# Preparing the weights of a four-layer graph network in pieces among the first turns

## The chip, the cores and the metric

The kernel runs on one core of a Trainium2 chip. The metric is the device time of one execution in microseconds (us); less is better. The core has a matrix engine (TensorE, here PE), and VectorE (DVE), ScalarE (ACT) and GpSimd (POOL) for everything else. SyncE (SP) issues the DMAs. Each engine works through its own list of instructions in order, and they meet at semaphores.

## The reference, cut to what matters

128 graphs of 128 nodes with 512 features each go through four layers of graph attention. Each layer normalises, takes the positive part, computes attention scores between nodes under a mask from `adj`, takes a softmax, multiplies by it, and adds the result to `x`:

```python
# layer 0:  one head; scores from h @ (W.T a1), h @ (W.T a2)
h = jnp.maximum(_layernorm(x), 0.0);  x = x + elu(softmax(masked(leaky(f1 + f2.T))) @ h)
# layer 1:  two GAT layers: 512 -> 4 heads x 256 (W1, att_src1, att_dst1, b1), elu,
#           then 1024 -> 512, one head (W2, att_src2, att_dst2, b2)
h = jnp.maximum(_layernorm(x), 0.0);  x = x + gat(elu(gat(h, W1, ...)), W2, ...)
# layer 2:  one head, additive attention with attn_w_src, attn_w_dst, attn_b
# layer 3:  8 heads of 64: xp = h @ W_proj; a_src, a_dst = xp . W_att; relu(att @ xp)
```

The weights `W1`, `W2` and `W_proj` are the same for all graphs.

## The kernel before

**Turns.** The kernel is a software pipeline that somebody wrote out by hand. A loop runs over `G + SKEW` turns (`G` = 128 graphs, `SKEW` = 12). In turn `step` each engine runs a fixed list of stages, and a stage called with `t.graph(k)` works on graph `step - k`, if there is one. So graph 0 is loaded in turn 1, meets its layer 0 in turns 2 to 4, its projection by `W1` in turns 4 and 5 (`L1a`), the one by `W2` in turn 6 (`L1b`), layer 2 in turns 7 and 8, the projection by `W_proj` in turn 10 (`L3`), and is stored in turn 12. The order in which an engine runs the stages of a turn is the order of the lines in its loop. Nothing is rearranged later.

**The weights.** They arrive in 16 chunks of 128 rows: chunks 0 to 3 are `w1` (1024 columns), 4 to 11 `w2` (512 columns), 12 to 15 `w3`, which is `W_proj` (512 columns). A chunk is loaded into a staging buffer by `stage_weights` (SP), and then prepared by a `split_weights` on each of three engines:

- DVE multiplies it with the attention vectors and sums, which gives the extra columns `ext`: a dot product (an instruction with its read of the accumulator behind it) for each head and vector. That is 8 for a `w1` chunk (256 wide), 2 for `w2` (512 wide), 16 for `w3` (64 wide).
- ACT copies the chunk to its rounded half `w_hi`, then waits for `ext_made` and copies `ext` also.
- POOL waits for both copies, subtracts them (`w_lo`), and raises `w_split`.

`split_weights(t)` stands first in a turn on each of the three engines. It prepares the chunks in `prepared[t.step]`: before, chunks 0 to 3 in turn 0, 4 to 11 in turn 1, 12 and 13 in turn 2, 14 and 15 in turn 3. The dot products put their products into `scratch`, which is the buffer that the scores of layer 0 use too, and so wait for `st_made0` as well. The staging buffers (`stage`, `stage3`, `att1`, `att2`, `att3`) are buffers of later layers that are still free: `xl` and `g1` of layer 1, `eE`, `pE`, `pTE` and `t_all["L3"]` of layer 3.

**What stands around it.** `load` (SP) brings `x` and `adj` of a graph. `norm_0` (ACT, lines 768 and 778) normalises it, `columns_L0` (DVE, 1112) makes the two score columns, `send_L0` and `spread_L0` (SP, 261 and 283) send the targets through DRAM to all partitions, `masked_L0` (POOL), `leaky_L0`, `exp_L0` (ACT) follow, `turn_exp_L0` and `product_L0` (PE, 396 and 409) turn the result and multiply. `pT_L0` (ACT, 811) copies it from PSUM between these two, and is the first stage of a turn on ACT. `residual_L0` (DVE, 1171) adds `x`. `project_L1a_high` and `_low` (PE, 365) follow `product_L0` on PE, and `values_L1a` (DVE, 1226, `xl`) follows these.

Before the loops, PE multiplies `a0_w` (1 MB) with the vectors of layer 0; POOL's first instruction waits for `setup_pool`, which `offdiag` raises in DVE's `make_rows`, behind the split of turn 0.

Of the kernel before, what the change touches and what calls it, by code (L numbers as in the profile page):

```python
# [1533 lines left out]
```

## Time and profile before

| | us |
|---|---|
| median of 3 runs | 3216.89 (3214.66 to 3220.53) |
| the profiled execution | 3215.87 |
| its span | 3213.9 |
| PE busy | 3052.3 (95%) |
| DVE, ACT, POOL busy | 2436.3, 2413.6, 2116.7 |
| granted TensorE clock, mean | 0.976 |
| `adj_in`, median from issue to landing (page, part 6) | 2.6 |

In the page's picture of 40 slices PE is at 1 in the first slice of 80 us, at 6 and 8 in the next two, at 9 up to the last two. So the kernel has a start, a long even part, and an end.

### The profile page before, as it was taken

What the parts mean: (1) busy time and instruction counts of PE and PEld (TensorE: products, weight loads), DVE (VectorE), ACT (ScalarE), POOL (GpSimd) and SP (SyncE); (2) the same over time, 40 slices, a digit from 0 to 9 for tenths busy, and PEclk for the clock granted to TensorE, in tenths of its full rate; (3) what the DMA queues carried; (4) which work ended last, traced back from release to release, by engine and by line L of the source; (5) the groups of instructions that cost most, each with busy time, mean ns of one, the idle gap of its engine ahead of it and who ended that gap; (6) DMA issues with size and microseconds to landing.
All of it is one profiled execution on the core that took longest, in us unless ns stands there. A gap on an engine that the chain in (4) does not pass through costs nothing.

```text
span 3213.9 us, 77726 instructions
## 1 busy us (share of the span) xinstructions
PE 3052.3 (95%) x21776; PEld 2809.7 (87%) x21776; DVE 2436.3 (76%) x5995; ACT 2413.6 (75%) x6561; POOL 2116.7 (66%) x3236
## 2 busy tenths in 40 slices
PE   1689999999999999999999999999999999999984
PEld 0579999999999999999999999999999999999974
DVE  6477877878787787878778787887878788787752
ACT  2467778878787787877878787887878788787753
POOL 4346666766666676766767666666766677676643
PEclk6899999999999999999999999999999999999986
DMA  4112222222222222222222222222212222222211
GB/s 135 32 46 62 78 63 74 66 64 76 63 78 63 69 71 62 78 63 78 63 69 71 62 78 63 77 64 67 74 62 78 63 75 65 69 72 62 66 39 44
DMA packets 170069, 217.14 MB, mean 68 GB/s; under 512 B 34864, under 2 KB 100528, under 8 KB 169648
## 3 DMA queue, kind: packets, MB, share of 16 engines
q1 hardware_dynamic: 169648, 212.18, 22.2%
q8 instruction: 184, 3.01, 0.4%
q14 instruction: 237, 1.94, 0.2%
HBM read 177.55 MB, written 34.54 MB: 66 GB/s over the span
## 4 chain that ended last, share of the span: by engine, by line
PE 91%; issue 4%; DVE 1%; POOL 1%; ACT 1%; DMA 0%; POOLq 0%; DVEq 0%; ACTq 0%
PE bank_c L365 23%; PE bank_b L365 22%; PE bank_e L365 11%; PE bank_e L691 8%; PE bank_b L513 7%; PE bank_a L409 3%; PE bank_e L655 3%; PE bank_c L591 3%; PE bank_a L435 3%; PE bank_b L507 2%; PE bank_b L358 2%; PE bank_e L358 2%; PE bank_a L396 0%; PE bank_a L422 0%; PE bank_c L579 0%
## 5 line engine op out<-in xcount | busy, mean ns | idle before, releaser
L365 PE MATMUL bank_b<-w_hi,hT_hi 128*128 128x344 f32 x1536 | 470.1, 360 | 7.2 <-DVE hT_lo L1215 6.7
L365 PE MATMUL bank_c<-w_hi,g_hi 128*128 128x258 f32 x2048 | 413.2, 283 | 2.4 <-DVE x L1171 2.4
L365 PE MATMUL bank_c<-w_lo,g_hi 128*128 128x258 f32 x2048 | 413.2, 283 | 0.0
L365 PE MATMUL bank_b<-w_lo,hT_hi 128*128 128x344 f32 x1536 | 410.2, 321 | 0.0
L1474 POOL TENSOR_TENSOR eE<-eE,nmE 128x512 f32<-128x512 f32 x256 | 266.2, 1040 | 178.0 <-DVE nmE L1289 177.0
L1467 POOL TENSOR_TENSOR eE<-t_all_L,mask 128x512 f32<-128x512 f32 x256 | 349.0, 1384 | 32.3 <-DMA t_all_L<-t_dram_L 31.5
L1455 POOL TENSOR_TENSOR g_lo<-g,g_hi 128x512 fp32r<-128x512 f32 x128 | 193.9, 1515 | 262.0 <-ACT g_hi L901 262.0
L365 PE MATMUL bank_c<-w_hi,g_lo 128*128 128x258 f32 x2048 | 363.8, 289 | 0.7
L940 ACT ACTIVATE eE<-eE,st 128x128 f32<-128x128 f32 x1024 | 326.1, 391 | 40.5 <-POOL eE L1467 40.4
L365 PE MATMUL bank_b<-w_hi,hT_lo 128*128 128x344 f32 x1536 | 347.2, 321 | 0.0
L365 PEld LDWEIGHTS bank_b<-w_hi,hT_hi 128*128 128x128 f32 x1536 | 277.7, 189 | 75.0 <-issue 67.1
L365 PEld LDWEIGHTS bank_c<-w_hi,g_hi 128*128 128x128 f32 x2048 | 322.8, 190 | 3.2 <-issue 3.2
L768 ACT ACTIVATE h<-x,rs 128x512 f32<-128x512 f32 x384 | 311.1, 811 | 14.0 <-POOL rs L1386 11.0
L365 PEld LDWEIGHTS bank_c<-w_lo,g_hi 128*128 128x128 f32 x2048 | 318.0, 190 | 0.0
L1383 POOL TENSOR_TENSOR rs<-rs,nhalf 128x1 f32<-128x1 f32 x512 | 289.8, 566 | 42.7
L1381 POOL TENSOR_SCALAR rs<-mv 128x1 f32<-128x1 f32 x512 | 113.0, 221 | 310.5 <-DVE mv L1071 278.6
L365 PE MATMUL bank_e<-w_hi,hT_hi 128*128 128x264 f32 x1024 | 300.6, 309 | 6.2 <-DVE rE L1314 6.2
L365 PEld LDWEIGHTS bank_c<-w_hi,g_lo 128*128 128x128 f32 x2048 | 289.5, 189 | 9.7 <-DVE g_lo L1258 4.3
L1112 DVE CUSTOM_DVE_ANT_0 product<-h,t_row 128x512 bf16<-128x512 f32 x256 | 295.0, 1152 | 0.0
L513 PE MATMUL bank_b<-pTB,xl 128*128 128x128 f32 x2048 | 275.4, 278 | 4.1 <-ACT pTB L880 4.1
L365 PE MATMUL bank_e<-w_lo,hT_hi 128*128 128x264 f32 x1024 | 276.7, 285 | 0.0
L365 PEld LDWEIGHTS bank_b<-w_lo,hT_hi 128*128 128x128 f32 x1536 | 274.2, 189 | 0.0
(136 smaller groups left out, 8785.5 us busy)
## 6 DMA issues: line engine op xcount, KB each, us to landing
t_all_L<-t_dram_L SPq DMA_DIRECT2D x128, 512.0 KB, 3.9
x_in<-in_x SPq DMA_DIRECT2D x128, 256.0 KB, 2.5
t_all_L1a<-t_dram_L1a SPq DMA_DIRECT2D x128, 256.0 KB, 4.3
out<-out_sb SPq DMA_DIRECT2D x128, 256.0 KB, 4.2
t_all_L<-t_dram_L SPq DMA_DIRECT2D x256, 64.0 KB, 2.9
adj_in<-in_adj SPq DMA_DIRECT2D x128, 64.0 KB, 2.6
t_dram_L1a<-t_rows_L1a SPq DMA_DIRECT2D x512, 0.5 KB
t_all_L1b<-t_dram_L1b SPq DMA_DIRECT2D x128, 64.0 KB, 2.8
```

The lines of the kernel that those rows point to most:

```text
L358: last = nc.tensor.transpose(bank[:, c * P:(c + 1) * P], src[:, c * P:(c + 1) * P], ident[:])
L365: last = mm(bank[:, 0:width], a[:, c * P:(c + 1) * P], w[:, c, b * width:(b + 1) * width], start=(first and c == chunks[0] and n == 0), st ...
L513: last = mm(bank_b[:, i, at * P:(at + 1) * P], xl[:, c * P:(c + 1) * P], pTB[:, c * P // F1, :], start=(at == 0), stop=(at == C1 // 2 - 1))
L691: last = mm(bank_e[:, i, k * KA:k * KA + NMIN], pTE[:, head, :], xa[:, head * KA:head * KA + NMIN], start=True, stop=True)
L768: activation(h[layer][:], src, ACT.Relu, bias=rs[layer][:, 2:3], scale=rs[layer][:, 1:2])\
L940: last = activation(eE[:, k, :], eE[:, k, :], ACT.Prelu, bias=st3[:, 0, k:k + 1], alpha=SLOPE)
L1112: last = nc.vector.tensor_tensor_reduce(product[:, layer + i, :], h[layer][:], row[layer][:], 1.0, first, ALU.mult, ALU.add, col)
L1381: ts(v, mv[layer][:, 1:2], EPS, None, ALU.add).then_inc(sem(f"var_made{layer}"), 1)
L1383: tt(r, v, nhalf[:], ALU.pow).then_inc(sem(f"rstd_made{layer}"), 1)
L1455: tt(g_lo[:, half, :], g1[:, half, :], g_hi[:, half, :].bitcast(F32), ALU.subtract)\
L1467: tt(eE[:, half, :], t_all["L3"][:, half, :], m, ALU.add).then_inc(sem(f"L3_masked{i}"), 1)
L1474: tt(eE[:, half, :], eE[:, half, :], nm, ALU.add).then_inc(sem(f"L3_shifted{i}"), 1)
```

## The change

The change does four things.

1. All stages run one turn earlier (`SKEW` = 11, each `t.graph(k)` becomes `t.graph(k - 1)`). Graph 0 is loaded before the loop.
2. The chunks are spread over more turns: 0 to 3 in turn 0, 4 and 5 in turn 1, 6 and 7 in turn 2, 8 to 11 in turn 3, and one of 12 to 15 in each of the turns 5 to 8. SP issues their loads by a table of its own (`fetched`).
3. They are staged in buffers of layer 3 (`eE`, `t_all["L3"]`, `pE`, `pTE`), but for chunks 2 and 3; so two waits of layer 1 for `W2_DONE` become `W1_DONE`.
4. The loads before the loop come in another order (`ident` and `a0_w` first), and `identb` and `offdiag` are made before the split.

```diff
-SKEW = 12
+SKEW = 11
...
-        stage = [xl[:, 0:D1], g1[:].rearrange("p c n -> p (c n)"),
-                 eE[:].rearrange("p h n -> p (h n)"), t_all["L3"][:].rearrange("p h n -> p (h n)")]
+        wide3 = [w.rearrange("p h n -> p (h n)") for w in (eE[:], t_all["L3"][:], pE[:], pTE[:])]
+        stage1 = [wide3[0], wide3[1], xl[:, 0:D1], g1[:].rearrange("p c n -> p (c n)")]
+        stage2 = [w[:, i * D:(i + 1) * D] for w in wide3 for i in range(2)]
...
-        prepared = {0: range(0, C), 1: range(C, C + C1), 2: range(C + C1, C + C1 + C // 2),
-                    3: range(C + C1 + C // 2, len(w_chunks))}
-        staged = [stage[n % WR] if n < C + C1 else stage3[n - C - C1] for n in range(len(w_chunks))]
+        prepared = {0: range(0, C), 1: range(C, C + 2), 2: range(C + 2, C + 4), 3: range(C + 4, C + C1),
+                    5: range(C + C1, C + C1 + 1), 6: range(C + C1 + 1, C + C1 + 2),
+                    7: range(C + C1 + 2, C + C1 + 3), 8: range(C + C1 + 3, C + C1 + C)}
+        fetched = {1: range(C + 4, C + 5), 2: range(C + 5, C + 7), 3: range(C + 7, C + C1),
+                   4: range(C + C1, C + C1 + 1), 5: range(C + C1 + 1, C + C1 + 3), 6: range(C + C1 + 3, C + C1 + C)}
+        staged = stage1 + stage2 + stage2[0:C]
...
-                    if kind == "w2":
+                    if n >= WR:
                         sp.wait_ge(sem("w_split"), n - WR + 1)
-                    if kind == "w3":
-                        sp.wait_ge(sem("w_split"), C + C1)
                     if n == C + C1:
+                        sp.wait_ge(sem("w_split"), C + 6)
...
-            spread(att1[1][:, 0:D1], row(att_src1.rearrange("h f -> (h f)")), "att1_in")
-            spread(att1[0][:, 0:D1], row(att_dst1.rearrange("h f -> (h f)")), "att1_in")
-            stage_weights(range(0, 1))
-
+            sp.dma_start(ident[:], ident_in).then_inc(sem("ident_loaded"), 16)
...
+            spread(att1[1][:, 0:D1], row(att_src1.rearrange("h f -> (h f)")), "att1_in")
+            spread(att1[0][:, 0:D1], row(att_dst1.rearrange("h f -> (h f)")), "att1_in")
+            stage_weights(range(0, 1))
+            load_graph(0, 0)
             stage_weights(range(1, C))
...
                 t = Turn(G, step)
-                if t.step == 1:
-                    load_rest()
-                if t.step in prepared and t.step:
-                    stage_weights(prepared[t.step])
-                spread_L3(t.graph(11))
...
-                load(t.graph(1))
+                if t.step == 0:
+                    stage_weights(range(C, 2 * C))
+                stage_weights(fetched.get(t.step, ()))
+                spread_L3(t.graph(10))
...
+                load(t.graph(0))
...
                     if g.i == 0:
-                        act.wait_ge(sem("w_split"), W2_DONE)
+                        act.wait_ge(sem("w_split"), W1_DONE)
...
             dve.wait_ge(sem("ext_zero"), 1)
+            dve.wait_ge(sem("ident_loaded"), 16)
+            nc.vector.tensor_copy(identb[:], ident[:]).then_inc(sem("setup_pe"), 1)
+            ts(offdiag[:], ident[:], -1.0, 1.0, ALU.mult, ALU.add).then_inc(sem("setup_pool"), 1)
...
-                    dve.wait_ge(sem("st_made0"), t.graph(3).made(1))
+                    dve.wait_ge(sem("st_made0"), t.graph(2).made(1))
```

The first place is ACT's list around `norm_0` of graph 0 (`h<-x_in`) and the first `pT_L0` (`pT_L`). Before:

```order
L761 ACTIVATE w_hi<-pE 128x2x256 [waits w_in3]
L763 ACTIVATE w_hi<-ext 128x2x8 [waits ext_made]
L768 ACTIVATE h<-x_in,rs 128x512 [waits L0_out,rs_made0]
L799 ACTIVATE e_L<-e_L,st 128x128 [waits L0_masked]
L805 ACTIVATE p_L,sum_L<-e_L,nm_L 128x128 [waits L0_recip,L0_turned,L0_max]
L811 ACTIVATE pT_L<-bank_a 128x128 [waits L0_out,L0_turned]
```

The same place of the changed kernel:

```order
L762 ACTIVATE w_hi<-ext 128x4 [waits ext_made]
L767 ACTIVATE h<-x_in,rs 128x512 [waits L0_out,rs_made0]
L798 ACTIVATE e_L<-e_L,st 128x128 [waits L0_masked]
L804 ACTIVATE p_L,sum_L<-e_L,nm_L 128x128 [waits L0_recip,L0_turned,L0_max]
L760 ACTIVATE w_hi<-pE 128x512 [waits w_in0]
L762 ACTIVATE w_hi<-ext 128x4 [waits ext_made]
L760 ACTIVATE w_hi<-pE 128x512 [waits w_in1]
L762 ACTIVATE w_hi<-ext 128x4 [waits ext_made]
L760 ACTIVATE w_hi<-pTE 128x512 [waits w_in2]
L762 ACTIVATE w_hi<-ext 128x4 [waits ext_made]
L760 ACTIVATE w_hi<-pTE 128x512 [waits w_in3]
L762 ACTIVATE w_hi<-ext 128x4 [waits ext_made]
```

`norm_0` of graph 0 had 16 chunks ahead of it and now has 8; four chunks now stand between the exponential and the copy `pT_L`, which follows them.

The second place is the border to the turn in which PE first projects by `W2` (turn 6 before, turn 5 now), on ACT. Before:

```order
L893 ACTIVATE g<-g 128x512 [waits elu_exp0]
L811 ACTIVATE pT_L<-bank_a 128x128 [waits L0_out,L0_turned]
L901 ACTIVATE g_hi<-g 128x512 [waits L1b_xl,g_made_last]
L901 ACTIVATE g_hi<-g 128x512 [waits L1b_first_high,g_made_first]
L768 ACTIVATE h<-x_in,rs 128x512 [waits L0_out,rs_made0]
```

And of the changed kernel:

```order
L892 ACTIVATE g<-g 128x512 [waits elu_exp0]
L760 ACTIVATE w_hi<-eE 128x2x256 [waits w_in0]
L762 ACTIVATE w_hi<-ext 128x2x8 [waits ext_made]
L810 ACTIVATE pT_L<-bank_a 128x128 [waits L0_out,L0_turned]
L900 ACTIVATE g_hi<-g 128x512 [waits L1b_xl,g_made_last]
L900 ACTIVATE g_hi<-g 128x512 [waits L1b_first_high,g_made_first]
L767 ACTIVATE h<-x_in,rs 128x512 [waits L0_out,rs_made0]
```

A chunk of `w3`, with its wait for DVE's dot products, has come between the turns; the same stands in the three turns behind.

The third place is SP's list behind the sending of graph 0's targets of `L1a`. Before:

```order
L269 DMA t_dram_L1a<-t_rows_L1a 4x32 x3
L283 DMA t_all_L1a<-t_dram_L1a 128x512 [waits L1a_masked,L1a_sent]
L254 DMA x_in<-in_x 128x512 [waits mask_made,x1_made]
```

And of the changed kernel:

```order
L269 DMA t_dram_L1a<-t_rows_L1a 4x32 x3
L224 DMA pE<-in_L_gnn_W_att 128x8x64 [waits w_split]
L224 DMA pE<-in_L_gnn_W_att 128x8x64
L226 DMA eE<-in_L_gnn_W_proj 128x512
L283 DMA t_all_L1a<-t_dram_L1a 128x512 [waits L1a_masked,L1a_sent]
L230 DMA x_in<-in_x 128x512 [waits mask_made,x1_made]
```

Three loads now stand ahead of the spread `t_all_L1a` of graph 0.

## Rows read from the trace of the kernel before

**Rows 1.** Busy time by stretch: us, then busy us and count by engine, granted clock

```profile
254.00:3088.00 2834.00, 2832.77 (x20534) 2625.02 (x20532) 2248.16 (x5414) 2254.70 (x6151) 1961.94 (x3004) 1.00 0.23 69
```

**Rows 2.** The chain that ended last, first 260 us: start, us, what

```profile
24.00 55.77 issue
...
142.55 0.86 PE bank_a L409 x2
...
163.95 0.99 PE bank_a L409 x2
...
186.16 0.86 PE bank_a L409 x2
```

**Rows 3.** Timeline, turn 0: start, us, engine, line, operation, [idle before, releaser]

```profile
13.37 0.42 DVE L1041 CUSTOM_DVE_ANT_0 product<-g,pE 128x256 bf16<-128x256 f32 x1 [2.72 <-DMA g<-in_L_gnn_W]
...
16.14 0.08 DVE L1041 DVE_READ_ACCUMULATOR2_ANT ext<- 128x1 f32 x1
...
22.87 2.34 POOL L1372 TENSOR_TENSOR w_lo<-xl,w_hi 128x1024 fp32r<-128x1024 f32 x1 [22.44 <-DVE offdiag L1053]
```

**Rows 4.** DMAs of the first 60 us: size, median us from issue to landing

```profile
ident<-in_ident SPq DMA_DIRECT2D x1, 64.0 KB, 6.8
```

**Rows 5.** Timeline, turn 1, dot products of `w2` beside POOL's subtractions

```profile
28.15 2.53 DVE L1041 CUSTOM_DVE_ANT_0 product<-xl,h 128x512 bf16<-128x512 f32 x1 [4.16 <-DMA xl<-in_L_gnn_W]
...
34.80 1.53 DVE L1041 CUSTOM_DVE_ANT_0 product<-eE,h 128x512 bf16<-128x512 f32 x1
...
37.08 1.53 DVE L1041 CUSTOM_DVE_ANT_0 product<-t_all_L,h 128x512 bf16<-128x512 f32 x1
```

**Rows 6.** Timeline, turn 3, `norm_0` of graph 0 on ACT

```profile
70.43 0.80 ACT L768 ACTIVATE h<-x_in,rs 128x512 f32<-128x512 f32 x1
```

**Rows 7.** Timeline, border of turns 3 and 4, DVE's last and PE's first

```profile
79.70 0.16 DVE L1166 RECIPROCAL sum_L<-sum_L 128x1 f32<-128x1 f32 x1
...
80.73 2.05 PE L409 MATMUL bank_a<-h,pT_L 128*128 128x512 f32 x2 [0.52 <-ACT pT_L L811]
```

**Rows 8.** Timeline, one `w3` chunk: its load, and its dot products on DVE

```profile
51.07 1.01 SPq L224 DMA_DIRECT2D pTE<-in_L_gnn_W_att  x2
...
56.59 0.23 DVE L1041 CUSTOM_DVE_ANT_0 product<-eE,pTE 128x64 bf16<-128x64 f32 x1 [7.46 <-DMA eE<-in_L_gnn_W_proj]
...
58.92 0.09 DVE L1041 DVE_READ_ACCUMULATOR2_ANT ext<- 128x1 f32 x1
```

**Rows 9.** Timeline, turn 5, the targets of `L1a` of graph 0

```profile
97.64 0.34 SPq L283 DMA_DIRECT2D t_all_L1a<-t_dram_L1a  x1
...
100.88 1.23 DVE L1226 TENSOR_TENSOR xl<-bank_b,b_row 128x1032 f32<-128x1032 f32 x1 [1.72 <-issue]
101.06 1.16 POOL L1442 TENSOR_TENSOR eB<-t_all_L1a,mask_turned 128x512 f32<-128x512 f32 x1 [9.37 <-DMA t_all_L1a<-t_dram_L1a]
```

**Rows 10.** Timeline, border of turns 5 and 6

```profile
120.73 1.10 PE L409 MATMUL bank_a<-h,pT_L 128*128 128x512 f32 x2 [1.61 <-ACT pT_L L811]
121.01 0.15 DVE L1166 RECIPROCAL sum_L<-sum_L 128x1 f32<-128x1 f32 x1
```

**Rows 11.** Timeline, DVE's last instruction of the turns 6, 7 and 8

```profile
142.77 0.75 DVE L1171 SCALAR_TENSOR_TENSOR x<-bank_c,sum_L1b,x 128x512 f32<-128x512 f32 x1 [0.77 <-PE bank_c L591]
...
164.80 0.75 DVE L1171 SCALAR_TENSOR_TENSOR x<-bank_c,sum_L1b,x 128x512 f32<-128x512 f32 x1
...
186.60 0.75 DVE L1171 SCALAR_TENSOR_TENSOR x<-bank_c,sum_L1b,x 128x512 f32<-128x512 f32 x1
```

**Rows 12.** Busy time by stretch, start and end of the kernel; granted clock after POOL's

```profile
114.00:118.00 4.00, 4.00 (x16) 4.00 (x16) 0.76 (x3) 0.79 (x3) 0.00 (x0) 0.50 0.02 4
...
122.00:126.00 4.00, 4.00 (x28) 4.00 (x28) 3.30 (x6) 0.75 (x1) 2.41 (x3) 1.00 0.36 102
...
3092.00:3096.00 4.00, 1.64 (x11) 1.63 (x11) 3.20 (x6) 2.11 (x7) 3.53 (x3) 0.89 0.32 111
3096.00:3100.00 4.00, 4.00 (x26) 4.00 (x25) 2.26 (x4) 3.06 (x9) 2.70 (x4) 0.68 0.07 16
```

More of the change, by code:

```diff
@@ L748, in _ @@
-                product_L2(t, t.graph(8))
-                turn_exp_L1b(t, t.graph(6))
-                project_L3_first(t, t.graph(10))
-                turn_exp_L0(t, t.graph(3))
+                product_L1b(t, t.graph(6))
+                product_L0(t, t.graph(3))
+                project_L1a_high(t, t.graph(4))
+                project_L1a_low(t, t.graph(4))
+                project_L1b_first_high(t, t.graph(5))
+                turn_h3(t, t.graph(9))
+                project_L1b_first_low(t, t.graph(5))
@@ new lines, in _ @@
+                project_L1b_last(t, t.graph(5))
+                turn_exp_L3_last(t, t.graph(10))
+                turn_exp_L3_first(t, t.graph(10))
+                turn_prob_L1a(t, t.graph(4))
+                product_L3_last(t, t.graph(10))
+                product_L3_first(t, t.graph(10))
+                product_L1a_last(t, t.graph(4))
+                turn_h1(t, t.graph(3))
+                turn_mask(t, t.graph(3))
+                project_L3_last_high(t, t.graph(9))
+                project_L3_last_low(t, t.graph(9))
@@ L753, in _ @@
+                turn_exp_L2(t, t.graph(7))
+                project_L1a_last(t, t.graph(3))
+                product_L1a_first(t, t.graph(4))
+                product_L2(t, t.graph(7))
+                turn_exp_L1b(t, t.graph(5))
+                project_L3_first(t, t.graph(9))
+                turn_exp_L0(t, t.graph(2))
         @block.scalar
@@ L1050, in make_rows @@
                 if t.step == 0:
-                    dve.wait_ge(sem("ident_loaded"), 16)
-                    nc.vector.tensor_copy(identb[:], ident[:]).then_inc(sem("setup_pe"), 1)
-                    ts(offdiag[:], ident[:], -1.0, 1.0, ALU.mult, ALU.add).then_inc(sem("setup_pool"), 1)
                     dve.wait_ge(sem("u0_made"), 1)
@@ L1347, in _ @@
-                rows_L3(t.graph(10))
-                recip_L2(t.graph(8))
-                most_L0(t.graph(3))
-                most_L1b(t.graph(6))
-                rows_L1a(t.graph(4))
-                elu_L1a_last(t.graph(5))
-                stats_0(t.graph(1))
-                residual_L2(t.graph(8))
-                recip_L1b(t.graph(6))
-                elu_L1a_first(t.graph(5))
-                recip_L0(t.graph(3))
-                columns_L2(t.graph(7))
-                residual_L1b(t.graph(6))
+                rows_L2(t.graph(7))
@@ new lines, in _ @@
+                sources_L3(t.graph(10))
+                residual_L0(t.graph(3))
+                columns_L0(t.graph(2))
+                values_L1a(t.graph(4))
+                moments_0(t.graph(1))
+                g_lo_first(t.graph(5))
+                rows_L0(t.graph(2))
+                most_L3_last(t.graph(10))
+                most_L1a(t.graph(4))
+                most_L3_first(t.graph(10))
+                hT_lo_L3(t.graph(9))
+                stats_1(t.graph(3))
+                recip_L1a(t.graph(4))
@@ new lines, in _ @@
+                moments_1(t.graph(3))
+                stats_3(t.graph(8))
+                rows_L1b(t.graph(5))
+                values_L1b(t.graph(5))
+                stats_2(t.graph(6))
+                recip_L3(t.graph(10))
+                result_L3(t.graph(10))
+                most_L2(t.graph(7))
+                moments_3(t.graph(8))
+                moments_2(t.graph(6))
+                hT_lo_L1a(t.graph(3))
+                rows_L3(t.graph(9))
+                recip_L2(t.graph(7))
+                most_L0(t.graph(2))
@@ L1361, in _ @@
+                most_L1b(t.graph(5))
+                rows_L1a(t.graph(3))
+                elu_L1a_last(t.graph(4))
+                stats_0(t.graph(0))
+                residual_L2(t.graph(7))
+                recip_L1b(t.graph(5))
+                elu_L1a_first(t.graph(4))
+                recip_L0(t.graph(2))
+                columns_L2(t.graph(6))
+                residual_L1b(t.graph(5))
         @block.gpsimd
```

195 lines of the change are left out of this document (73 added, 122 removed).

## The prediction, made before the changed kernel ran

> **What bounds the kernel now.** I read the busy time by stretch first. From 254 to 3088 us PE is busy for 2832.77 of 2834.00 us at a full clock [rows 1]. Nothing that the change does reaches into that part: after turn 8 every engine has the list that it had, and what is computed per graph is the same. So only the start can pay, and a microsecond by which the even part begins earlier is a microsecond of the span. The chain of waits shows the start next: after the weights' first dot products it has 55.77 us of "issue" that end with graph 0's first use of PE, near 80 us [rows 2]. There the engines DVE, ACT and POOL prepare 16 chunks, and the first `norm_0` waits behind all of them. Behind it the pipeline fills: the chain passes through `product_L0` (bank_a L409) once per turn, at 142.55, 163.95 and 186.16, that is every 21.4 to 22.2 us. These turns are bound by one loop over PE, DVE, ACT and POOL, which PE's in-order list closes: `product_L0`, `project_L1a`, `xl`, softmax, `product_L1a`, then the next `product_L0`. So what is put at the head of such a turn is paid in full. I take each step in the order of time and keep a balance: by how much the changed kernel is ahead of the one before at the same stage.
>
> **1. The first `norm_0` comes earlier: +25.0 us.** Before, it starts at 70.43 [rows 6]. The new time has to be built up. Chunk 0 now stands behind `ident`, `a0_w`, two `att` rows: with itself 2.56 MB. The same bytes were on their way until `ident` had landed, issued at about 5.3 and 6.8 us on its way [rows 4]: so 12.0. The 8 dot products of a `w1` chunk take 16.22 - 13.37 = 2.85 us, and POOL's subtraction 2.34 [rows 3]. Before, POOL started when `offdiag` was made, at 22.87, behind all four; now it can start with chunk 0 and meets the dot products of chunk 1. How the two get on is shown only for `w2`: a dot product of 0.6 us took 2.53 us beside a subtraction of POOL's, later ones 1.53, and a chunk cost 37.08 - 34.80 = 2.28 us, which is two dot products (1.2) and one subtraction of half the width (1.1) in a row [rows 5]. They take turns. So a `w1` chunk beside a subtraction costs 2.85 + 2.34 + 0.1 = 5.3: the dot products of chunk 3 end at 12.0 + 2.9 + 3 x 5.3 = 30.8. The copies of `s_row` and `t_row` and `stats_0` follow (three instructions over 512 columns of one input, about 1.9), POOL has chunk 3 until 33.4, chunks 4 and 5 end at 37.4. Then a new wait: SP loads graph 1 behind the load of chunk 8, which waits for chunk 4's subtraction (37.2). With three issues (1.0) and 2.6 us of landing, `stats_0` of graph 1 stands until 40.8, and chunks 6 and 7 stand behind it on DVE: 0.7 + 1.3 + 2.28 more, 45.1, and ACT's `norm_0` at 45.4. The gain is 70.4 - 45.4 = 25.0. Bounds: if the two did not meet on `w1`, 3 x 2.4 = 7.2 us earlier, and graph 1 with it; if each landing takes 2 us more, 4 less. So +21 to +32.
>
> The Trainium skill (SBUF — State Buffer, "SBUF: two separate sides") says that VectorE with two inputs in SBUF and GpSimd hold a shared port pair for a whole instruction, and that the other blocks. By that rule the 256-wide dot products block as the 512-wide ones do and `norm_0` starts at 45.4; by the durations of `w1` alone it would start at about 38. The trace agrees with the rule for `w2` (2.53 us for 0.6) and does not show `w1`.
>
> **2. Four chunks before the first `pT_L0`: -8.1 us.** Before, DVE is free at 79.86 and `product_L0` starts at 80.73, its wait being for `pT_L` [rows 7]. Now ACT has chunks 8 to 11 between, and each small copy waits for the dot products. DVE starts them at its 79.86 (in the time of before): 1.3 + 3 x 2.28 = 8.1 until 88.0; then ACT's small copy (0.2), `pT_L` (0.3) and two hand-overs, 0.75 together. 88.8 instead of 80.73. Nothing hides it: PE has nothing else. Bounds: 5.5 (POOL not in the way: 4 x 1.3 + 0.75 from 79.86, with 0.4 of waits) to 9. Balance +16.9.
>
> **3. Three loads ahead of graph 0's `t_all_L1a`: -2.2 us.** Before, its spread was issued at 97.64 and POOL began with it at 101.06, 3.4 us later; `xl` was ready at 102.11 and POOL's `eB` at 102.22, so there is no slack [rows 9]. Now 0.75 MB stand ahead, issued 0.5 us beyond the old time. Before, the same 0.75 MB from its first issue (51.07) to its use (56.59) took 5.5 us [rows 8]; issued at 96.8 it is down at 102.3, and the spread's 0.25 MB about 1 us behind: 103.3. So 2.2 late, between 0.5 (only the issue) and 3.5. In the turns behind, less stands ahead of the spread (0.5 and 0.25 MB), and what step 4 adds to the side of `xl` covers it. Balance +14.7.
>
> **4. One `w3` chunk at the head of four turns: -16.9 us.** Its 16 dot products take 59.01 - 56.59 = 2.42 us [rows 8]. ACT cannot copy `pT_L0` before the chunk's small copy, and that waits for DVE, which comes to the chunk only after its last work of the turn before. So `product_L0` starts at DVE's free time + 2.42 + 0.75:
> - turn 6: DVE free at 121.16: 124.3 instead of 120.73 [rows 10], 3.6 late;
> - turn 7: `residual_L1b`, which itself waits for PE's `product_L1b`, ends at 143.52 [rows 11]: 146.7 instead of 142.55 [rows 2], 4.1 late;
> - turn 8: 165.55: 168.7 instead of 163.95, 4.8 late;
> - turn 9: 187.35: 190.5 instead of 186.16, 4.4 late.
>
> (Turns numbered as before; now 5 to 8.) `project_L1a` and `xl` stand behind `product_L0` on PE, so the loop is longer by all of it. POOL's subtraction (about 1.4) then delays `g_lo_last` and meets the score columns on DVE; by my count these are done just as `project_L1a` is, so no more is added. Bounds: 9.7 (only the dot products, 4 x 2.42) to 20. Balance -2.2.
>
> **5. The clock: -6 us.** At the end of the kernel PE idles for 2.4 of 4 us, and the granted clock of these 4 us is 0.89 and of the next 0.68 [rows 12]: (0.11 + 0.32) x 4 / 0.5 = 3.4 us at 1.2 GHz. In the filling turns it has so far stayed at 2.4 GHz, with idle times like the 1.61 us ahead of `product_L0` in [rows 10]. Now 4 us of idle stand ahead of `product_L0`. I expect the clock to fall in each of the four turns, just as the 24 matmuls of `project_L1a` come. At the low level 4 us hold 16 matmuls, at the high one 28 [rows 12], so 3.4 us cost 1.5: 4 x 1.5 = 6. Bounds: 0 (never falls) and 4 x 2.6 = 10.4 (all 24 at the low level, 6.0 instead of 3.4 us). I take the nearer row, that of the end. Balance -8.2.
>
> The edits that cost nothing: fewer buffers shared with layer 1 removes two waits that ended long before; the renumbering itself moves nothing, since the loop of a turn is in the same order and an empty first turn costs no time.
>
> So the sum is 3215.87 + 8.2 = 3224.1 us against the profiled execution, which lies 1.0 under the median of the three runs; against the median, 3225.
>
> **The rivals.**
> - *The clock stays up.* The filling turns of before hold 2.4 GHz although PE idles ahead of `product_L0` in each [rows 10]. Then step 5 goes: 3216.9 + 2.2 = 3219, no change that can be told. Against it: the fall after 2.4 us at the end.
> - *The four pieces hide.* DVE, ACT and POOL are all under 80% busy, and if the dot products ran while DVE waits for something, or ACT had slack before `pT_L0`, step 4 would cost nothing and step 5 with it: +14.7, 3202 us, faster. The point from which it decides is (25.0 - 8.1 - 2.2 - 6.4) / 4 = 2.1 us per turn: under that, faster. Against it: `product_L0` started 0.4 to 0.5 us behind `pT_L`, in line, and the dot products alone are 2.42.
> - *The start gains more.* If `w1` is not slowed by POOL, +7.2: 3218, no change; with the clock up as well, 3212.
> - *The clock stays down for longer*, and the loads take 2 us more: -10.4 instead of -6, and -4: 3233.
>
> **How the numbers follow.** This measurement can tell 0.2%, 6.4 us, from no change. The forecast (8.2 us slower) has 0.45; since it lies near the limit, a third of it falls to "same". The clock up: 0.20. More gain at the start: 0.12, nearly all "same". The pieces hide: 0.12, faster. The clock down for longer: 0.11. Slower: 0.30 + 0.11 + 0.04 = 0.45; faster: 0.12 + 0.02 = 0.14; same: 0.41. The range leaves out the hidden pieces and half of the last case: 3210 to 3234. The forecast's own range is 3219 to 3231.
>
> **What would show it.** In the changed kernel's timeline: POOL's first subtraction begins near 15 us and each dot product of `w1` that follows one takes over 2 us (step 1); `norm_0` of graph 0 at 45.4, `product_L0` of graph 0 at 63.8 (step 2), POOL's first `eB` at 86 (step 3). ACT's small copies of `w3` have idle times of about 2 us before them, ended by DVE, and the chain's bank_a L409 comes every 25 to 27 us in the four turns, then every 22 (step 4). The granted clock shows four dips in these turns (step 5). The even part and the end look as before. The prediction is wrong if `norm_0` comes before 40 or after 50 us, if the turns with a chunk are under 2 us longer, or if the even part's turn has changed.

## The result, and the profile after

| | kernel before | changed kernel |
|---|---|---|
| median, lowest and highest of 7 runs, us | 3215.83 (3211.90 to 3220.53) | 3228.32 (3224.86 to 3230.92) |
| ratio, 95% interval | 1 | 1.0039 (1.0027 to 1.0051) |
| span of the profiled execution, us | 3213.9 | 3229.0 |
| mean granted clock of PE | 0.976 | 0.973 |

The changed kernel is 12.5 us, 0.39%, slower. Its busy row for the even part, of the same length as [rows 1] (us, then busy us and count by engine, PE first, granted clock, DMA):

```profile
268.00:3102.00 2834.00, 2832.21 (x20529) 2624.49 (x20528) 2248.26 (x5410) 2253.91 (x6148) 1963.87 (x3004) 1.00 0.23 68
```

PE is as full as before: the difference is made in the first 268 us. Turn 0 first: SP's issues of chunk 0 and of graph 0's mask, DVE's dot products, POOL (start, us, engine, line, operation, idle before and its releaser), as an answer to [rows 3 to 5]:

```profile
4.95 0.66 SPq L226 DMA_DIRECT2D eE<-in_L_gnn_W  x1
...
6.52 0.94 SPq L231 DMA_DIRECT2D adj_in<-in_adj  x1
```

```profile
14.93 0.43 DVE L1043 CUSTOM_DVE_ANT_0 product<-eE,pE 128x256 bf16<-128x256 f32 x1 [11.90 <-issue]
...
18.26 2.56 DVE L1043 CUSTOM_DVE_ANT_0 product<-t_all_L,pE 128x256 bf16<-128x256 f32 x1
...
23.39 2.56 DVE L1043 CUSTOM_DVE_ANT_0 product<-xl,pE 128x256 bf16<-128x256 f32 x1
```

```profile
18.19 2.35 POOL L1371 TENSOR_TENSOR w_lo<-eE,w_hi 128x1024 fp32r<-128x1024 f32 x1 [17.77 <-ACT w_hi L762]
```

A `w1` chunk costs 23.39 - 18.26 = 5.13 us, because one of its dot products lasts as long as POOL's subtraction beside it. Then the wait for graph 1, `norm_0` of graph 0 [rows 6] and `product_L0` of graph 0 [rows 7]:

```profile
43.38 0.69 DVE L1063 BATCH_NORM_STATS2 bn<-x_in 128x6 f32<-128x512 f32 x1 [3.44 <-DMA adj_in<-in_adj]
```

```profile
47.94 0.80 ACT L767 ACTIVATE h<-x_in,rs 128x512 f32<-128x512 f32 x1
```

```profile
66.95 2.05 PE L408 MATMUL bank_a<-h,pT_L 128*128 128x512 f32 x2 [9.06 <-ACT pT_L L810]
```

Between these two stand ACT's small copies for the chunks 8 to 11, 2.5 us apart, each waiting for DVE:

```profile
63.87 0.20 ACT L762 ACTIVATE w_hi<-ext 128x4 fp32r<-128x4 f32 x1 [1.77 <-DVE ext L1043]
...
66.37 0.21 ACT L762 ACTIVATE w_hi<-ext 128x4 fp32r<-128x4 f32 x1 [1.77 <-DVE ext L1043]
```

The changed kernel is ahead by 22.5 us at `norm_0` and by 13.8 at `product_L0`. In turn 4, the targets of `L1a`, against [rows 9]:

```profile
87.48 1.23 DVE L1225 TENSOR_TENSOR xl<-bank_b,b_row 128x1032 f32<-128x1032 f32 x1 [1.72 <-issue]
```

```profile
84.38 1.25 SPq L226 DMA_DIRECT2D eE<-in_L_gnn_W_proj  x1
85.72 0.38 SPq L283 DMA_DIRECT2D t_all_L1a<-t_dram_L1a  x1
```

```profile
90.09 1.15 POOL L1441 TENSOR_TENSOR eB<-t_all_L1a,mask_turned 128x512 f32<-128x512 f32 x1 [12.23 <-DMA t_all_L1a<-t_dram_L1a]
```

The lead is 13.4 at `xl`, as before the loads, and 11.0 at `eB`. In the four turns with a `w3` chunk, ACT first (at the head of turn 5), then PE's `product_L0` of the four turns and of the first one behind them, against [rows 2, 10]:

```profile
111.89 0.21 ACT L762 ACTIVATE w_hi<-ext 128x16 fp32r<-128x16 f32 x1 [2.63 <-DVE ext L1043]
112.01 0.26 ACT L810 ACTIVATE pT_L<-bank_a 128x128 f32<-128x128 f32 x1
```

```profile
112.47 2.05 PE L408 MATMUL bank_a<-h,pT_L 128*128 128x512 f32 x2 [4.97 <-ACT pT_L L810]
...
140.14 2.04 PE L408 MATMUL bank_a<-h,pT_L 128*128 128x512 f32 x2 [3.91 <-ACT pT_L L810]
...
168.26 2.05 PE L408 MATMUL bank_a<-h,pT_L 128*128 128x512 f32 x2 [4.54 <-ACT pT_L L810]
...
196.27 2.04 PE L408 MATMUL bank_a<-h,pT_L 128*128 128x512 f32 x2 [4.13 <-ACT pT_L L810]
...
221.05 1.02 PE L408 MATMUL bank_a<-h,pT_L 128*128 128x512 f32 x2
```

ACT's small copy waits for the last dot product, `pT_L` stands behind it, and PE stands 3.9 to 5.0 us for `pT_L`; then its first matmuls take 2.05 us instead of 1.02. The busy rows around these four places tell why (columns as in [rows 12], the clock is the third number from the end):

```profile
108.00:112.00 4.00, 0.00 (x0) 0.00 (x0) 3.08 (x34) 1.34 (x4) 0.00 (x0) 0.72 0.55 196
112.00:116.00 4.00, 3.53 (x8) 2.53 (x9) 1.24 (x2) 2.12 (x5) 3.72 (x4) 0.50 0.00 1
136.00:140.00 4.00, 0.23 (x1) 0.00 (x0) 3.08 (x33) 0.45 (x3) 0.05 (x1) 0.64 0.26 99
140.00:144.00 4.00, 3.86 (x10) 2.86 (x11) 1.22 (x2) 1.78 (x3) 3.92 (x5) 0.51 0.01 2
164.00:168.00 4.00, 0.00 (x0) 0.00 (x0) 3.85 (x38) 0.33 (x3) 0.00 (x0) 0.55 0.17 48
...
196.00:200.00 4.00, 3.73 (x9) 2.73 (x10) 1.48 (x2) 1.92 (x4) 3.83 (x5) 0.50 0.01 2
```

PE does nothing for a stretch, the granted clock falls to 0.50 (1.2 GHz), and the matmuls of `project_L1a` begin at the low level. Ahead of the second, third and fourth of these places the clock had been at 1.00 (2.4 GHz); ahead of the first it was still coming up (0.70 in the 4 us from 104 on).

### The profile page after: what moved, and what is told of

It is laid out like the page before. It is cut to its first block, busy times and chain, and to the rows that moved or that the text cites. A ratio compares the mean times of both kernels' runs of the same rounds, so it can differ in the third digit from the quotient of the medians.

```text
span 3229.0 us, 77688 instructions
## 1 busy us (share of the span) xinstructions
PE 3059.8 (95%) x21776; PEld 2813.8 (87%) x21776; DVE 2436.4 (75%) x5995; ACT 2413.5 (75%) x6561; POOL 2115.6 (66%) x3236
## 4 chain that ended last, share of the span: by engine, by line
PE 91%; issue 3%; DVE 2%; POOL 1%; ACT 1%; DMA 0%; POOLq 0%; DVEq 0%; ACTq 0%
PE bank_b L364 22%; PE bank_c L364 22%; PE bank_e L364 11%; PE bank_e L690 8%; PE bank_b L512 7%; PE bank_a L408 4%; PE bank_e L654 3%; PE bank_a L434 3%; PE bank_c L590 3%; PE bank_b L506 2%; PE bank_b L357 2%; PE bank_e L357 2%; PE bank_a L421 0%; PE bank_a L395 0%; PE bank_c L578 0%
```

## The experiments

Each kernel has a column of marks from its own trace: `norm_0` of graph 0, `product_L0` of graphs 0, 1 and 2 and of the first graph behind the `w3` chunks (graph 6), and the five intervals from graph 1 to graph 6. The last column leaves out what the first 80 us cost. Its first interval, from graph 1 to graph 2, scatters by itself: 26.2 to 30.6 us in the changed kernel, e6, e9, e10 and e11, with the clock. From graph 2 to graph 6 these five agree within 0.5 us (108.5 to 109.0), so a statement on the four turns is best read from there. All rows below that of the changed kernel are edits of it, but for e10.

| kernel | us, median | ratio to before (95%) | `norm_0` | graph 0 | graph 1 | graph 2 | graph 6 | five intervals |
|---|---|---|---|---|---|---|---|---|
| before | | 1 | 70.43 | 80.73 | 95.81 | 120.73 | 208.28 | 112.5 |
| changed | 3228.3 | 1.0039 (1.0027 to 1.0051) | 47.94 | 66.95 | 82.36 | 112.47 | 221.05 | 138.7 |
| e1, `w3` in turn 3 | 3220.2 | 1.0004 (0.9995 to 1.0012) | 47.11 | 82.62 | 98.03 | 123.12 | 210.40 | 112.4 |
| e2, PE kept busy | 3220.1 | 1.0008 (0.9999 to 1.0016) | 45.98 | 65.11 | 80.08 | 108.81 | 209.12 | 129.0 |
| e3, ACT's copies later | 3215.4 | 0.9991 (0.9982 to 1.0000) | 45.99 | 65.11 | 80.52 | 105.59 | 204.12 | 123.6 |
| e4, every engine later | 3215.8 | 0.9997 (0.9988 to 1.0007) | 47.78 | 66.95 | 82.39 | 107.51 | 206.40 | 124.0 |
| e5, dots cut in two | 3205.5 | 0.9963 (0.9950 to 0.9975) | 47.88 | 66.96 | 82.39 | 109.44 | 197.54 | 115.2 |
| e6, `w1` loaded first | 3223.0 | 1.0017 (1.0008 to 1.0025) | 41.26 | 60.37 | 75.77 | 106.36 | 215.32 | 139.6 |
| e7, all chunks in waits | 3188.2 | 0.9904 (0.9891 to 0.9918) | 35.90 | 45.70 | 61.84 | 87.92 | 176.01 | 114.2 |
| e8, e7 and e6 | 3180.5 | 0.9888 (0.9873 to 0.9904) | 31.28 | 41.09 | 56.76 | 82.28 | 170.37 | 113.6 |
| e9, fetch behind | 3231.3 | 1.0040 (1.0027 to 1.0054) | 45.97 | 65.15 | 80.56 | 106.76 | 215.22 | 134.7 |
| e10, changed, again | 3230.4 | 1.0033 (1.0020 to 1.0045) | 46.23 | 65.25 | 80.66 | 110.98 | 219.60 | 138.9 |
| e11, e9 again | 3228.3 | 1.0024 (1.0015 to 1.0033) | 45.91 | 65.11 | 80.52 | 110.65 | 219.51 | 139.0 |

The kernel before was run beside each call: its medians were 3218.0 for e1 to e4, 3217.5 for e5 to e8, 3217.8 for e9 and 3220.6 for e10 and e11, against 3215.8 beside the changed kernel. So two medians of different calls can differ by up to 5 us with no edit, and the ratio is the safer measure. The changed kernel has 7 runs, e5, e9 and e10 have 5, e7 and e8 have 4, the others 11.

**e1: `w3` in one block.**

```
-        prepared = {..., 3: range(C + 4, C + C1), 5: ..., 6: ..., 7: ..., 8: ...}
-        fetched = {..., 3: range(C + 7, C + C1), 4: ..., 5: ..., 6: ...}
+        prepared = {..., 3: range(C + 4, C + C1 + C)}
+        fetched = {..., 3: range(C + 7, C + C1 + C)}
```

> The changed kernel with one table altered: all four chunks of w3 are prepared in turn 3, behind the last four of w2, instead of one each at the head of turns 5 to 8; nothing is computed differently. Theory T (a chunk at the head of a turn is paid in full, because ACT works in order and its copies wait for DVE's dots, and the clock falls behind it): the 16.5 us of chunk time and the 8.0 us of lowered clock that turns 5 to 8 lose in the changed kernel are gone, and turn 3 pays four times about 3.6 us, 14.4 us, instead. The balance against the kernel before is then about -1 to -3.5 us at turn 5 and stays there; time about 3218 us, 10 us under the changed kernel, and product_L0 in the turns 5 to 9 comes every 22 to 26 us as in the kernel before. Theory P (the pieces are cheap where they stand, and the loss is made elsewhere): the block of turn 3 is the dearer place, and the time is at or above the changed kernel's 3228 us. Theory S (the loss is in the first 100 us: w1 beside POOL, the order of the loads): within 3 us of the changed kernel.

As theory T has it: the five intervals are those of the kernel before (112.4 against 112.5), turn 3 pays 16.5 us (`product_L0` of graph 0 stands 35.5 us behind `norm_0`, 19.0 in the changed kernel), and at graph 6 the kernel is 2.1 us behind the one before. The four heads are the place of the loss: theories P and S fall. Not quite all of it lies there: `fetched` takes the three loads of the prediction's step 3 out of turn 4 too, so their 2.4 us go with the heads.

**e2: keep PE busy.**

```
                 product_L1b(t, t.graph(6))
+                if 5 <= t.step <= 8:
+                    for k in range(24):
+                        mm(bank_e[:, k % 2, 0:B1], w1_hi[:, k % C, 0:P], w1_hi[:, k % C, 0:B1], start=True, stop=True)
                 product_L0(t, t.graph(3))
```

> The changed kernel with 24 matmuls added on TensorE in each of turns 5 to 8, between product_L1b and product_L0, of w1's high parts with themselves into a bank that is unused then; their results are read by nobody. They fill the idle time in which TensorE waits for pT_L0 (row: 0 to 0.23 of the 4 us ahead of product_L0). The chunks stay where they are. Theory T with the clock as an own term of 8.0 us: TensorE's granted clock stays at or near 1.00 behind the fill (0.50 to 0.60 in the changed kernel), product_L0 starts no later than in the changed kernel, and each of the four turns gets back 1.4 to 2.7 us: about 3220 us. Theory N (the falls of the clock in these turns cost nothing, since other engines end last there): 3228 us, with the clock up. Theory W (24 matmuls, 24 times about 0.25 us, outlast the wait): product_L0 starts later by up to 2 us a turn, and the gain is between none and 8 us less 4 times that excess.

Busy rows of e2 around two of the four places:

```profile
108.00:112.00 4.00, 3.19 (x17) 2.74 (x18) 2.04 (x8) 2.23 (x5) 3.38 (x4) 1.00 0.05 6
...
160.00:164.00 4.00, 3.43 (x18) 2.99 (x19) 2.31 (x5) 2.21 (x5) 3.63 (x4) 1.00 0.14 20
```

The clock stays at 1.00, and PE works more but ends sooner. From graph 2 to graph 6 the changed kernel takes 221.05 - 112.47 = 108.6 us, e2 209.12 - 108.81 = 100.3: the clock alone is 8.3 us, and the median is 8.2 lower. The chunks, still at the heads, keep their price. Theory N falls, and with it the prediction's rival that the clock stays up.

**e3: only ACT's part is moved.**

```
-                split_weights(t)
+                if t.step < 5:
+                    split_weights(t)
                 pT_L0(t.graph(3))
                 ...
                 norm_0(t.graph(2))
+                if t.step >= 5:
+                    split_weights(t)
```

> The changed kernel with one call moved on ACT alone: in turns 5 to 8 the copies of the w3 chunk stand behind norm_0 instead of at the head of the turn; DVE's dots and POOL's subtractions stay at the head. Theory T (the price of a chunk at the head is ACT waiting in order for DVE's dots, ahead of pT_L0, on which TensorE waits): pT_L0 no longer waits for the dots; the turn loses at most what DVE's own 2.5 us put ahead of its row work cost, so 0 to 2 us for each of four instead of 3.3 to 4.8, and TensorE has no gap long enough for the clock to fall: about 3208 to 3216 us. Rival D (DVE's 2.5 us at the head, and not ACT's wait, is what delays the chain): the chunk costs as before, each turn 3.3 to 4.8, the clock falls as before, about 3228 us. Rival Q (POOL, whose subtraction now waits for ACT's copies behind norm_0, becomes late with its part of the turn): slower than the changed kernel, with TensorE waiting for POOL in turns 5 to 8.

The time is at the upper end of what theory T gave, and rival Q has its part in that. Who waited for whom in e3 from 125 to 210 us (total, times, longest):

```profile
POOL w_lo L1374 <- ACT w_hi L762: 23.9, 3, 8.0
ACT eB L862 <- POOL eB L1444: 14.7, 3, 4.9
...
PE bank_c L364 <- DVE g_lo L1260: 8.1, 3, 3.0
```

PE waits no longer for `pT_L` than in the kernel before (1.60 us ahead of graph 2's product), but POOL, whose subtraction still heads its turn, stands for ACT's later copy, and the masked scores `eB` behind it come late. The first of these three waits is as long in the changed kernel (25.0 us in the same stretch); in place of the second, ACT waits for `xl` both there and in the kernel before, and the third is not among PE's waits in either. So the head of a turn must be cleared on all three engines.

**e4: all three engines' parts are moved into the turn.**

```
 DVE:   moments_2(t.graph(6)); + split_weights(t); hT_lo_L1a(t.graph(3))
 ACT:   + split_high(t); pT_L3_last(t.graph(10)) ... + split_ext(t); elu_first(t.graph(4))
 POOL:  scale_3(t.graph(8)); + split_weights(t)
```

> The changed kernel with the same four chunks of w3 in the same turns 5 to 8, but each engine's part put where that engine is idle: DVE's dots behind moments_2, ACT's two copies ahead of pT_L3_last and ahead of elu_first, POOL's subtractions behind scale_3. The same work is done. Theory T: the 16.5 us at the heads and the 8.0 us of clock go, so that the lead of about 11 to 12 us over the kernel before that the changed kernel has at turn 5 (with its first chunk not yet paid) is kept to the end: 3203 to 3206 us, 23 to 25 us under the changed kernel and 10 to 13 us under the kernel before. Theory P (whatever place it has, a chunk's 2.5 us on DVE and 1 us on ACT delay the turn, since these engines have no idle time that is not needed): 3 to 4 us a turn remain, 3218 to 3228 us. Theory S (the loss is in the first 100 us): no different from the changed kernel.

This theory missed by 10 us, and the trace shows where (DVE, then PE, then the busy row behind):

```profile
169.68 0.69 DVE L1231 TENSOR_TENSOR hT_lo<-bank_b,hT_hi 128x512 fp32r<-128x512 f32 x1
```

```profile
170.69 0.63 PE L364 MATMUL bank_b<-w_hi,hT_hi 128*128 128x344 f32 x1 [2.10 <-DVE hT_lo L1231]
```

```profile
172.00:176.00 4.00, 4.00 (x18) 4.00 (x18) 1.39 (x3) 0.00 (x0) 1.28 (x2) 0.50 0.00 0
```

The 16 dot products stood ahead of `hT_lo`, for which PE waits, so the same two losses came back at another place: 2.1 us of waiting, and the clock behind it. PE waits for `hT_lo` three times from 125 to 210 us, 6.7 us in all, and from graph 2 to graph 6 the kernel takes 98.9 us, where the one before takes 87.6. I had called this place of DVE idle without looking at what stands behind it.

**e5: the same, with a chunk's 16 dot products cut into 7 and 9**, each in a wait of DVE.

```
 DVE:   stats_1(t.graph(3)); + dots(t, 7 of 16); recip_L1a(t.graph(4))
        result_L3(t.graph(10)); + dots(t, 9 of 16); most_L2(t.graph(7))
```

> The changed kernel with the four chunks of w3 in turns 5 to 8 as before, ACT's copies and POOL's subtractions placed as in e4, but DVE's 16 dots of a chunk cut in two: seven behind stats_1 (DVE stands 1.12 us there for ACT's exponentials) and nine ahead of most_L2 (1.46 us there). In e4 all 16 stood ahead of hT_lo_L1a, and the intervals of product_L0 were 23.6, 26.7 and 27.0 us where the kernel before has 21.5, 22.1 and 22.3: TensorE waited 2.1 to 2.2 us for hT_lo, and its clock was at 0.50 behind that. Theory T2 (what counts is not whose head of line a chunk stands in, but whether its 2.5 us of dots fit into time in which DVE waits anyway): TensorE's wait for hT_lo goes back to under 0.3 us, the clock stays up, the intervals are those of the kernel before, and the lead of 11 to 13 us is kept: 3203 to 3207 us. Rival O (the engines are so full in these turns that 2.5 us of dots cost 2 us a turn wherever they stand): as e4, 3214 to 3218 us. Rival G (a gap that DVE has for ACT is on the chain, and dots in it push the reciprocal behind it by more than their overhang, with POOL's and TensorE's share of the heads in its wake): between the two, 1 us a turn, 3208 to 3211 us.

```profile
162.80 0.08 DVE L1083 DVE_READ_ACCUMULATOR2_ANT ext<- 128x1 f32 x1
163.05 0.18 DVE L1283 RECIPROCAL sumB<-sumB 128x4 f32<-128x4 f32 x1 [0.17 <-DVE ext L1083]
...
168.14 0.69 DVE L1260 TENSOR_TENSOR hT_lo<-bank_b,hT_hi 128x512 fp32r<-128x512 f32 x1 [0.27 <-ACT hT_hi L868]
```

```profile
172.00:176.00 4.00, 3.01 (x11) 1.35 (x9) 3.47 (x11) 3.41 (x7) 1.73 (x3) 1.00 0.19 56
```

Seven dot products end as ACT's exponentials do, `hT_lo` is back to waiting for ACT, and the clock is 1.00. The same work now costs next to nothing: graph 2 to graph 6 takes 88.1 us, the kernel before 87.6. The kernel is 22.8 us faster than the changed one, and 12.0 faster than the one before. Rivals O and G fall. Two things differ from e4, the cut and the place; whether all 16 would have fitted uncut in one of these waits was not run.

**e6: `w1` is loaded first.**

```
             sp.dma_start(ident[:], ident_in)...
+            spread(att1[1]...); spread(att1[0]...); stage_weights(range(0, 2))
             ... st3, a0_w ...
-            spread(att1[1]...); spread(att1[0]...); stage_weights(range(0, 1))
             load_graph(0, 0)
-            stage_weights(range(1, C))
+            stage_weights(range(2, C))
```

> The changed kernel with the order of the loads at the start altered alone: w1's attention rows and its chunks 0 and 1 are issued right behind ident, ahead of the two columns and four blocks of layer 0's weights; all else is unchanged. Chunk 0's dots began at 15 us in the changed kernel, where the prediction had put chunk 0's landing at 12.0. Theory T (the order of issue on SP, 0.4 to 0.9 us each, sets when the first dots start, and w1's dots are the chain up to 33 us): the first dots begin at 7.5 to 9 us, norm_0 of graph 0 comes 6 to 7 us earlier than the changed kernel's 47.9, and the time falls by as much, to about 3222 us. Rival B (layer 0's own weights, now later, or the DMA queues' speed set the pace): TensorE's four u0 products and DVE's copies behind w1's dots come later than w1, or chunks 2 and 3 land late, and no more than 2 us is gained, 3226 to 3228 us.

```profile
8.36 0.42 DVE L1044 CUSTOM_DVE_ANT_0 product<-eE,pE 128x256 bf16<-128x256 f32 x1 [5.27 <-issue]
```

The first dot product begins 6.6 us earlier than in the changed kernel, `norm_0` 6.7, `product_L0` of graph 6 5.7, the time 5.3 (7 by the two ratios). Theory T holds, and layer 0's own weights still come in time. Part of the size is scatter: against e10, the same kernel once more, the first three are 4.3, 5.0 and 4.3.

**e7 and e8: all chunks in waits.** As e5, with `w2` treated likewise. Places on DVE, in halves of a chunk (e7; e8 has e6's order of loads in addition):

```
 turn 2: chunks 4, 5 behind rows_L0
 turn 3: 6 and half of 7 ahead of hT_lo_L1a; half of 7 and 8 ahead of rows_L1a
 turn 4: half of 9 at the head; half of 9 and half of 10 ahead of values_L1a; half of 10 and 11 ahead of hT_lo_L1a
 turns 5 to 8: w3 as in e5; graphs 0 and 1 are loaded at the start
```

> e5 with w2's eight chunks spread in the same manner: none in turn 1 nor in a block of turn 3, but two behind rows_L0 in turn 2 (DVE stands 5.8 us there for the targets of graph 0), and the other six in parts of one or two dots, 1.28 us each, in the waits of 2 to 6 us that DVE has in turns 3 and 4; both first graphs are loaded at the start. Loads of the last chunks stand behind the spreads on SP. Theory T2 (chunks in waits of DVE are free): norm_0 of graph 0 comes about 10 us earlier than in the changed kernel (37 to 38 us), product_L0 of graph 0 about 9 us earlier still (66.95 becomes 47 to 49), and the balance over the kernel before at turn 5 is 28 to 32 us; time 3185 to 3192 us. Rival L (the loads, which wait for POOL's subtractions in a ring of four, come late and hold SP, so that graph 0's sends stand behind them): gain of 5 to 10 us less, with SP's waits for w_split in turns 2 to 4. Rival O (the dots cost their 2.5 us wherever they stand): no better than e5.

> e7 with e6's order of the loads as well. Theory T: the gains add, 6 to 7 us on top of e7, norm_0 of graph 0 at about 31 us, time 3179 to 3186 us. Rival B (in e7 the u0 products, or the loads, end last ahead of norm_0 once w2 is gone from there): no more than 2 us under e7.

`norm_0` and `product_L0` of graph 0 in e8:

```profile
31.28 0.81 ACT L784 ACTIVATE h<-x_in,rs 128x512 f32<-128x512 f32 x1 [4.16 <-POOL rs L1455]
```

```profile
41.09 2.05 PE L415 MATMUL bank_a<-h,pT_L 128*128 128x512 f32 x2 [0.52 <-ACT pT_L L827]
```

From `norm_0` to `product_L0` 9.8 us, where the changed kernel has 19.0 and the one before 10.3: the `w2` chunks are gone from the chain. e7's time lies in the range of theory T2, and its `norm_0` and `product_L0` came 1 to 2 us ahead of it; rivals L and O fall. The gains add: 7.7 us from e7 to e8, where e6 alone gave 5.3, so rival B falls too. e8 beats both kernels: 3180.5 us, 1.12% (0.96 to 1.27) under the kernel before, and its even part is unchanged:

```profile
217.00:3051.00 2834.00, 2832.55 (x20524) 2624.26 (x20523) 2246.63 (x5408) 2253.44 (x6149) 1958.64 (x3003) 1.00 0.23 68
```

**e9 to e11: the loads of `w3` behind the broadcast.** e10 is the changed kernel, e11 is e9's.

```
-                stage_weights(fetched.get(t.step, ()))
+                if t.step < 4: stage_weights(fetched.get(t.step, ()))
                 spread_L3(t.graph(10)); store(t.graph(11)); spread_L1a(t.graph(4))
+                if t.step >= 4: stage_weights(fetched.get(t.step, ()))
```

> The changed kernel with one thing moved on SP's queue: from turn 4 on the loads of w3's rows and chunks stand behind spread_L3, store and spread_L1a instead of ahead of them. Theory T (step 3: the three loads ahead of the broadcast of t_all_L1a in turn 4 hold it back by 2.2 to 2.4 us, and POOL's eB waits for it): eB of graph 0 comes at about 87.7 instead of 90.09 us, the later turns keep that, and the time is 2.0 to 2.6 us under the changed kernel, about 3226 us. Rival K (xl, DVE's sum at 87.48 us, or POOL itself is next behind, so the broadcast is hidden): under 0.5 us. Rival D (the chunks now land later than DVE's dots want them at the head of turns 5 to 8): slower than the changed kernel, DVE waiting for a load there.

> The changed kernel itself once more, beside e11, so that e9's edit can be compared on the same chip at the same time. Every theory: 12 to 13 us over the kernel before, about 3229 to 3231 us on this scale.

> e9's kernel again. Its trace had eB of graph 0 2.3 us nearer to norm_0 than the changed kernel's and product_L0 4.0 us earlier against norm_0 in turns 5 to 8, yet its five times had a median of 13.5 us over the kernel before, where the changed kernel has 12.5. Theory T (the moved loads give 2 to 4 us and five times can't tell it): 2 to 4 us under e10. Rival D (the loads behind the spread cost elsewhere in executions other than the profiled one, as where a chunk lands late): at or above e10, and this trace, another execution, shows where.

POOL's `eB` and the busy row of the 4 us from 100 on, first in e9, then in e11:

```profile
85.84 1.15 POOL L1444 TENSOR_TENSOR eB<-t_all_L1a,mask_turned 128x512 f32<-128x512 f32 x1 [9.46 <-DMA t_all_L1a<-t_dram_L1a]
```

```profile
100.00:104.00 4.00, 1.79 (x15) 1.55 (x13) 2.33 (x8) 1.75 (x3) 0.00 (x0) 1.00 0.01 1
```

```profile
85.73 1.16 POOL L1444 TENSOR_TENSOR eB<-t_all_L1a,mask_turned 128x512 f32<-128x512 f32 x1 [9.71 <-DMA t_all_L1a<-t_dram_L1a]
```

```profile
100.00:104.00 4.00, 3.53 (x12) 3.56 (x13) 0.29 (x1) 1.36 (x4) 0.00 (x0) 0.50 0.02 4
```

The broadcast comes 2.3 us nearer to `norm_0` in both (39.9 and 39.8 us behind it, 42.15 in the changed kernel and in e10): step 3 of the prediction has its size. What becomes of it is not the same in the two executions. ACT's next work on `eB` needs POOL's result and `xl` as well; here it is in e9, then in e11, and then `xl` in e10:

```profile
87.03 1.28 ACT L865 ACTIVATE eB<-eB,xl 128x128 f32<-128x128 f32 x4 [4.45 <-POOL eB L1444]
```

```profile
88.82 1.28 ACT L865 ACTIVATE eB<-eB,xl 128x128 f32<-128x128 f32 x4 [5.35 <-DVE xl L1228]
```

```profile
87.61 1.23 DVE L1225 TENSOR_TENSOR xl<-bank_b,b_row 128x1032 f32<-128x1032 f32 x1 [2.64 <-issue]
```

In e11 ACT waited for `xl`, so the earlier broadcast was hidden but for 0.4 us: that is rival K. It is no exception. In the traces of the changed kernel and e2 `xl` begins 2.6 and 2.7 us ahead of `eB`, but in e10 and in e3 to e6, which have the same loads there, only 0.3 to 0.8 us ahead. In e9 the clock came up earlier (0.99 in the 4 us from 80 on, 0.50 in e10 and e11), `xl` was early and the gain was kept; the clock was up for `project_L1a_last` too, and graph 2's `product_L0` came 60.8 us behind `norm_0`. In e11 it was at 0.50 there, and it came at 64.7, as in e10 (64.8). The times: e9 no gain, against theory T; e11 2.1 us under e10, with intervals that overlap. e10 itself is 9.9 us over the kernel before, where 12 to 13 were expected. Rival D's late chunk shows in neither trace; whether the mean gain is 0 or 4 us these runs don't settle.

## Why the prediction was right, point by point

**Where the time is decided.** The even part did not change (2832.2 us of 2834 busy). By `product_L0` of graph 8 the changed kernel is 12.5 us behind (267.08 against 254.54), which is what the medians differ by; the trace's own 15.1 us of span has 2.6 us more, gathered over the long even part and the end.

**Step 1, +25.0, was +22.5.** The mechanism was right (5.13 us for a `w1` chunk against 5.3, and the wait for graph 1 with 3.44 us); the mis-sized term is chunk 0's landing, put at 12.0, measured at 14.9. It was taken from one landing in one trace, that of `ident` behind the same number of bytes. This landing scatters: in the ten traces that have the same issues up to chunk 0 (changed, e1 to e5, e7, e9 to e11) SP issues it at 4.95 or 4.96, and the first dot product begins at 12.4 to 15.0, with 13.2 in the middle. So the term was 1.2 us short, and the rest of the 2.9 is this execution. `norm_0` came at 45.9 to 47.9 in nine of them (e7 has other work ahead of it), a gain of 22.5 to 24.5. Where chunk 0 is late, SP's issues behind it are long too (0.83 and 0.94 us in the changed kernel, 0.46 and 0.43 in e10), but they stand behind it in SP's list, and what makes it late is not shown.

**Step 2, -8.1, was -8.7.** The step from 22.5 to 13.8; a chunk took 2.5 us, where 2.28 was written down.

**Step 3, -2.2, was -2.4** (13.4 ahead at `xl`, 11.0 at `eB`), and e9 and e11 take 2.3 of it back at `eB`. The prediction had "no slack" between `xl` and `eB`. That was so before, but where the clock is low `xl` comes late by itself, and then the loads put `eB` only 0.3 to 0.8 us behind it (e3 to e6, e10).

**Step 4, -16.9, was -16.4.** The balance at DVE's last work of a turn, less the balance at the `product_L0` behind it, gives 3.4, 4.1, 4.7 and 4.3, where 3.6, 4.1, 4.8 and 4.4 were written down. e1 takes the chunks away and the five intervals are those of before; e2 leaves them and takes away the clock.

**Step 5, -6, was -8.1 in the trace and -8.3 by e2.** The clock was low behind each of the four waits of 3.9 to 5.0 us. The mis-sized term is the price of a fall. It was taken from 3.4 us at the low level at the end of the kernel; here the busy rows give 6.8 us (from 136 on: (0.36 + 0.49) x 4 / 0.5), and a fall cost 1.6 to 2.6 us instead of 1.5 (the balance at a `product_L0` less the one at DVE's last work of its turn). The prediction's sentence that the clock had so far stayed at 2.4 GHz in the filling turns was wrong by its own rows: [rows 12] have 0.50 from 114 on. It holds from about 120 us on, which is where it was used.

So two terms were about 2 us off, both to the slow side, and no error made up for another. The measured steps add up to 13.1 us behind, where graph 6's `product_L0` has 12.8 and graph 8's 12.5; the prediction had 8.2. The turns with a chunk came after 27.7, 28.1, 28.0 and 24.8 us, where 25 to 27 was written down, since the clock took more. The stated range, 24 us wide, was easier to meet than the sum, and "same" and "slower" had nearly even chances.

The Trainium skill (SBUF — State Buffer, "SBUF: two separate sides") gives the rule that was weighed: by it a dot product with two inputs in SBUF waits out POOL's whole instruction, for 256 columns as for 512. By that rule the trace agrees: 2.56 us for one of 0.42 beside POOL's 2.35.

**The rivals.** That the pieces hide fell as the change stands: 4.1 us a turn, twice the 2.1 at which it would have decided. But what it said of the engines was true. They have the room, and e5 finds it: cut in two, the dot products fit in DVE's waits, and that is worth nearly the whole of steps 4 and 5. The prediction argued from "under 80% busy" against the head of the turn only, and rightly; it did not ask where the 20% lie.

## What to carry to other kernels

Before work is put into a pipeline's turn, list for each engine its waits, with what ends each and what stands behind it: a piece is free if it is shorter than the wait and nothing that another engine awaits is pushed back (e5), and it is paid in full, with the waits behind it, at the head of an in-order list (changed kernel, e3) or ahead of what another engine awaits (e4). Cut the work to the size of the waits (1.1 and 1.5 us here), rather than by its natural unit (2.5 us). And charge a new wait of PE twice, once for its length and once for the clock behind it (half as much again here: 8 us on 16.4).
